# Experts' first layer: two blocks' 64-channel parts side by side in the array's row halves, bias moved into the gelu

## The reference, cut to what matters

```python
xn2 = _layernorm(x, norm2_w, norm2_b).reshape(-1, C)      # 1152 x 192
logits = xn2 @ w_gate
top_vals, top_idx = jax.lax.top_k(logits, 2)
gates = softmax(top_vals)
def body(acc, p):                                          # for each of 8 experts
    w1, bb1, w2, bb2, g = p                                # w1 192 x 768, w2 768 x 192
    h = jax.nn.gelu(xn2 @ w1 + bb1, approximate=False)
    return (acc + g[:, None] * (h @ w2 + bb2), None)
```

## Time and profile before

| what | value |
|---|---|
| median of 3 runs (lowest, highest) | 395.0 us (394.66, 396.63) |
| the profiled execution: its time, its span | 395.83 us, 393.9 us |
| PE, weight loads (PEld), DVE, ACT, POOL busy | 321.1, 284.4, 226.4, 170.8, 82.3 us |
| mean granted clock of TensorE | 0.888 of full |
| chain that ended last, by engine | PE 63%, DVE 17%, DMA 7%, ACT 5% |
| experts' loop, from the first L1424 to the end of the span | 292.08 to 393.9 us |

### The profile page before, as it was taken

How to read it: one execution, slowest core, us unless ns; L and a number is a source line. 1 busy time by engine, 2 the same in 40 slices (tenths; PEclk the granted TensorE clock), 3 DMA queues, 4 the chain that set the end, 5 groups by cost and what they waited for, 6 DMA issues and landing times.

```text
span 393.9 us, 6349 instructions
## 1 busy us (share of the span) xinstructions
PE 321.1 (81%) x2177; PEld 284.4 (72%) x2177; DVE 226.4 (57%) x543; ACT 170.8 (43%) x408; POOL 82.3 (21%) x79
## 2 busy tenths in 40 slices
PE   8869506680979899999998896649599999999990
PEld 6849404460768797887986674639499999999980
DVE  1718998999989746553473875568422332322230
ACT  0154402404624277798847964116233333333320
POOL 9310002010000101010010000000405555554631
PEclk9989956796698999999999997557689999999996
DMA  8950000000000003443039588000222222222322
GB/s 279 360 146 0 1 0 0 0 2 0 1 2 1 0 2 95 122 135 84 24 80 262 165 206 237 17 22 1 55 86 42 42 41 43 42 40 42 51 23 22
DMA packets 20555, 27.27 MB, mean 69 GB/s; under 512 B 3458, under 2 KB 15570, under 8 KB 20522
## 3 DMA queue, kind: packets, MB, share of 16 engines
q1 hardware_dynamic: 16634, 22.80, 20.4%
q0 software_dynamic: 3888, 4.03, 7.0%
HBM read 22.05 MB, written 4.77 MB: 68 GB/s over the span
## 4 chain that ended last, share of the span: by engine, by line
PE 63%; DVE 17%; DMA 7%; ACT 5%; issue 4%; POOL 1%; SPq 1%; DVEq 0%; ACTq 0%; POOLq 0%
PE banks L1424 9%; PE banks L1214 9%; PE banks L1215 9%; PE banks L1411 7%; PE banks L1413 7%; PE banks L1284 6%; DMA vs<-v_scratch 4%; PE banks L1237 3%; ACT patch L757 2%; PE banks L1247 2%; DVE arena L979 1%; PE banks L1385 1%; PE banks L1335 1%; PE banks L1308 1%; PE banks L1208 1%
## 5 line engine op out<-in xcount | busy, mean ns | idle before, releaser
L579 POOL TENSOR_TENSOR rs<-va,consts 96x6 f32<-96x6 f32 (+1 forms) x16 | 17.8, 1114 | 222.8 <-DVE va L890 129.0
L833 ACT ACTIVATE ffn<-banks 128x384 f32<-128x384 f32 x40 | 19.6, 491 | 61.3 <-PE banks L1413 60.5
L600 POOL DMA_INDIRECT out<-s,ffn x20 | 32.4, 1620 | 49.5 <-DVE s L1175 41.3
L1424 PE MATMUL banks<-arena,ffn 128*128 x240 | 42.1, 326 | 0.0
L1175 DVE TENSOR_SCALAR s<-banks,ffn 128x192 f32<-128x192 f32 x20 | 8.3, 417 | 57.4 <-PE banks L1424 47.9
L1424 PEld LDWEIGHTS banks<-arena,ffn 128*128 128x128 f32 x240 | 38.5, 190 | 0.0
L1214 PE MATMUL banks<-ht,kvrw 128*128 128x288 f32 x40 | 17.9, 538 | 19.9 <-DVE h L876 14.7
L1247 PE MATMUL banks<-consts,xh 96*128 96x96 f32 (+1 forms) x96 | 12.9, 280 | 19.1 <-DVEq L914 17.8
L590 POOL DMA_INDIRECT vs<-xh_scratch,ffn x21 | 21.2, 1008 | 32.4 <-DVE ffn L1154 26.3
L1284 PE MATMUL banks<-rvw,ffn 128*96 128x192 f32 x144 | 26.4, 335 | 1.0 <-ACT ffn L729 1.0
L1214 PEld LDWEIGHTS banks<-ht,kvrw 128*128 128x128 f32 x40 | 9.5, 252 | 23.4 <-issue 17.8
(11 more groups left out here) (215 smaller groups left out, 756.2 us busy)
## 6 DMA issues: line engine op xcount, KB each, us to landing
arena<-in_w SPq DMA_DIRECT2D x8, 576.0 KB, 8.1
patch<-in_xp SPq DMA_DIRECT2D x12, 288.0 KB, 5.9
arena<-in_w1a SPq DMA_DIRECT2D x8, 384.0 KB, 6.3
vs<-v_scratch SPq DMA_DIRECT2D x24, 114.8 KB
arena<-in_w1b SPq DMA_DIRECT2D x8, 195.0 KB
v_scratch<-vt SPq DMA_DIRECT2D x4, 229.5 KB, 3.0
xh_scratch<-xh SPq DMA_DIRECT2D x4, 216.0 KB, 2.4
out<-h SPq DMA_DIRECT2D x1, 864.0 KB, 4.9
```

The costliest lines, as they stand in the source:

```text
L600: pool.indirect_dma_start(out[:, :], bass.IndirectOffsetOnAxis(ap=IS[:, j:j + 1], axis=0), YG[j % 2], None, compute_op=ALU.add).then_inc(s ...
L833: freed(A(HST[j % 2][:, 384 * i:384 * (i + 1)], ps[:, 0:384], ACT.Gelu), job)
L1424: ins = mm(ps[:, 0:C], HST[j % 2][:, 128 * k:128 * (k + 1)], W2[:, bass.ds(e, 1), C * k:C * (k + 1)], start=(k == 0), stop=(k == HB - 1))
```

## The change

The 64-channel parts of two hidden blocks (m and m + 3) lie in partitions 0 to 63 and 64 to 127 of W1B, and so do two copies of the tokens' last 64 channels in XT. `up` first makes all six 128-channel matmuls (now L1427), then three pairs of 64-channel matmuls (now L1432), one of each pair in rows 0 to 63 of the array and the other in rows 64 to 127, into the two banks. For the second copy the scratch rows are 256 channels wide (a second store per group), and the gathered rows too. The bias is loaded as 48 rows, transposed once by PE (job `b1`), copied with the weights (6 columns, behind the old tile's gelu), and added by six ACTIVATEs of 128 columns (now L841) in place of two of 384. The job `b1` moves all later jobs by one bank.

```diff
-                    load("w1b", W1B[0:C1 + 1, e, :], w1b[:, e, :])
+                    for r in range(2):
+                        load("w1b", W1B[C1 * r:C1 * (r + 1), e, :], w1b[0:C1, e, HID // 2 * r:HID // 2 * (r + 1)])
...
+                if n_experts < E and upto == E:
+                    load("b1", B1ROWS, w1b[C1, :, :].rearrange("e (m p) -> (e m) p", p=128))
...
-                    sp.dma_start(xh_dram[GT * g:GT * (g + 1), :].rearrange("(t p) c -> p t c", p=T),
-                                 XH[:, GTILES * (g % 2):GTILES * (g % 2 + 1), :]).then_inc(xh_stored[g], 16)
+                    sp.dma_start(rows[:, :, 0:C], xh).then_inc(xh_stored[g], 16)
+                    sp.dma_start(rows[:, :, C:256], xh[:, :, 128:C]).then_inc(xh_stored[g], 16)
...
-                freed(A(XT[j % 2][0:C1, 1, :], ps[0:C1, 128:256], ACT.Identity, bias=chan_("n2_b", 1), scale=chan_("n2_w", 1)), job)
+                freed(A(XT[j % 2][:, 1, :], ps[:, 128:256], ACT.Identity, bias=chan_("n2_b", 1, 0, 128), scale=chan_("n2_w", 1, 0, 128)), job)
...
-                    freed(A(HST[j % 2][:, 384 * i:384 * (i + 1)], ps[:, 0:384], ACT.Gelu), job)
+                    for m in range(3 * i, 3 * i + 3):
+                        ins = A(HST[j % 2][:, 128 * m:128 * (m + 1)], ps[:, 128 * (m % 3):128 * (m % 3 + 1)], ACT.Gelu,
+                                bias=WE[j % 2][:, HID + HID // 2 + m:HID + HID // 2 + m + 1])
+                    freed(ins, job)
...
-                ch.then(CP(we[:, 0:1, :], W1A[:, bass.ds(e, 1), :]))
-                ch.step(CP(we[0:C1 + 1, 1:2, :], W1B[0:C1 + 1, bass.ds(e, 1), :]))
+                ch.then(CP(we[:, 0:HID].unsqueeze(1), W1A[:, bass.ds(e, 1), :]))
+                ch.then(CP(we[:, HID:h1].unsqueeze(1), W1B[:, bass.ds(e, 1), :]))
+                if j >= 2:
+                    taken(dve, ("h", j - 2, 1))
+                ch.step(CP(we[:, h1:h1 + HB].unsqueeze(1), B1[:, bass.ds(e, 1), :]))
...
+            ps = full(dve, ("b1",))
+            freed(CP(B1.rearrange("p e m -> p (e m)"), ps[:, 0:E * HB]), ("b1",))
+            taken(dve, ("b1",))
...
+            pe.wait_ge(loaded["b1"], 16)
+            ps = begin(("b1",))
+            end(pe.transpose(ps[:, 0:E * HB], B1ROWS, ident[0:E * HB, 0:E * HB]), ("b1",))
...
-                for i in range(2):
-                    ps = begin(("h", j, i))
-                    for k in range(3):
-                        at_ = 384 * i + 128 * k
-                        h = ps[:, 128 * k:128 * (k + 1)]
-                        mm(h, WE[j % 2][:, 0, at_:at_ + 128], XT[j % 2][:, 0, :], start=True, stop=False)
-
-                        ins = mm(h, WE[j % 2][0:C1 + 1, 1, at_:at_ + 128], XT[j % 2][0:C1 + 1, 1, :], start=False, stop=True)
-                    end(ins, ("h", j, i))
+                we, xt = WE[j % 2], XT[j % 2]
+                ps = [begin(("h", j, i)) for i in range(2)]
+                for m in range(HB):
+                    mm(ps[m // 3][:, 128 * (m % 3):128 * (m % 3 + 1)], we[:, 128 * m:128 * (m + 1)], xt[:, 0, :], start=(m % 3 == 0), stop=False)
+
+                for k in range(3):
+                    for i in range(2):
+                        r = slice(C1 * i, C1 * (i + 1))
+                        ins = mm(ps[i][:, 128 * k:128 * (k + 1)], we[r, HID + 128 * k:HID + 128 * (k + 1)], xt[r, 1, :], start=False, stop=(k == 2))
+                        if k == 2:
+                            end(ins, ("h", j, i))
```

More of the change, by code:

```diff
@@ L158, in moe_jobs @@
 def moe_jobs():
-    out = [("rank",), ("gturn",)] + [("b2", t) for t in range(0, TILES, 2)] + [("list",)]
+    out = [("rank",), ("gturn",)] + [("b2", t) for t in range(0, TILES, 2)] + [("b1",), ("list",)]
     out += [("xt", 0), ("xt", 1), ("h", 0, 0), ("h", 0, 1)]
@@ L208, in build @@
         W1A = arena[:, 0:E * HID].rearrange("p (e n) -> p e n", e=E)
-        W1B = arena[:, E * HID:2 * E * HID].rearrange("p (e n) -> p e n", e=E)
+        W1B = arena[:, E * HID:E * HID + E * HID // 2].rearrange("p (e n) -> p e n", e=E)
+        B1ROWS = arena[0:E * HB, E * HID + E * HID // 2:E * HID + E * HID // 2 + 128]
+        B1 = arena[:, 2 * E * HID - E * HB:2 * E * HID].rearrange("p (e m) -> p e m", e=E)
         W2 = arena[:, 2 * E * HID:ARENA].rearrange("p (e n) -> p e n", e=E)
@@ L264, in build @@
         names = ["chan", "const", "tokw", "tokb", "kvrw", "wow", "kfw", "rfw", "vfw", "qkvw", "projw",
-                 "gatew", "b2", "w1a", "w1b", "w2"]
+                 "gatew", "b2", "w1a", "w1b", "b1", "w2"]
         loaded = {n: sem("loaded_" + n) for n in names}
@@ L356, in xh_free @@
                 if kk == "g":
-                    eng.wait_ge(xh_stored[gg], 16)
+                    eng.wait_ge(xh_stored[gg], 32)
         class Chain:
@@ L440, in fcarve @@
             return ffn[:, fat[0] - n:fat[0]]
-        XG = [vs_[:, C * i:C * (i + 1)] for i in range(3)]
+        XG = [vs_[:, 256 * i:256 * (i + 1)] for i in range(3)]
         YG = [S[:, i, 0:C] for i in range(2)]
@@ L449, in build @@
         HST = [fcarve(HID) for _ in range(2)]
-        WE = [x.rearrange("p (b n) -> p b n", b=2) for x in (rvw[:, :], fcarve(2 * HID))]
+        WE = [rvw[:, 0:HID + HID // 2 + HB], fcarve(HID + HID // 2 + HB)]
         v_dram = nc.dram_tensor("v_scratch", [TOK, NH * HW], F32).ap()
-        xh_dram = nc.dram_tensor("xh_scratch", [TOK, C], F32).ap()
+        xh_dram = nc.dram_tensor("xh_scratch", [TOK, 256], F32).ap()
         block = ctx.enter_context(nc.Block())
@@ L509, in _ @@
                     normalised(sp, step[1:])
-                    sp.dma_start(xh_dram[GT * g:GT * (g + 1), :].rearrange("(t p) c -> p t c", p=T),
-                                 XH[:, GTILES * (g % 2):GTILES * (g % 2 + 1), :]).then_inc(xh_stored[g], 16)
+                    rows = xh_dram[GT * g:GT * (g + 1), :].rearrange("(t p) c -> p t c", p=T)
+                    xh = XH[:, GTILES * (g % 2):GTILES * (g % 2 + 1), :]
+                    sp.dma_start(rows[:, :, 0:C], xh).then_inc(xh_stored[g], 16)
+                    sp.dma_start(rows[:, :, C:256], xh[:, :, 128:C]).then_inc(xh_stored[g], 16)
                 if kind == "vt":
@@ L584, in _ @@
             for g in range(G):
-                pool.wait_ge(xh_stored[g], 16)
+                pool.wait_ge(xh_stored[g], 32)
             def gather(j):
@@ L1134, in _ @@
             ch.then(dve.memset(O[:, 0, :], 0.0))
-            for j in range(2):
-                ch.then(dve.memset(XT[j][C1:C1 + 1, 1, :], 1.0))
             def weights(j):
@@ L1142, in weights @@
                 we = WE[j % 2]
-                ch.then(CP(we[:, 0:1, :], W1A[:, bass.ds(e, 1), :]))
-                ch.step(CP(we[0:C1 + 1, 1:2, :], W1B[0:C1 + 1, bass.ds(e, 1), :]))
+                h1 = HID + HID // 2
+                ch.then(CP(we[:, 0:HID].unsqueeze(1), W1A[:, bass.ds(e, 1), :]))
[3 more added lines that the diff above has]
+                ch.step(CP(we[:, h1:h1 + HB].unsqueeze(1), B1[:, bass.ds(e, 1), :]))
                 dve.sem_inc(we_ready, 1)
@@ L1149, in _ @@
             dve.wait_ge(loaded["w1a"], 16 * E)
-            dve.wait_ge(loaded["w1b"], 16 * E)
+            dve.wait_ge(loaded["w1b"], 32 * E)
+            ps = full(dve, ("b1",))
+            freed(CP(B1.rearrange("p e m -> p (e m)"), ps[:, 0:E * HB]), ("b1",))
+            taken(dve, ("b1",))
             weights(0)
@@ L1386, in _ @@
             end(ins, ("list",))
-            for n in ("w1a", "w1b", "w2"):
-                pe.wait_ge(loaded[n], 16 * E)
+            for n, k in (("w1a", 1), ("w1b", 2), ("w2", 1)):
+                pe.wait_ge(loaded[n], 16 * k * E)
             def tile_expert(j):
@@ L1398, in turn_tokens @@
                 pe.transpose(ps[:, 0:128], XG[j % 3][:, 0:128], ident)
-                end(pe.transpose(ps[0:C1, 128:256], XG[j % 3][:, 128:C], ident), ("xt", j))
+                end(pe.transpose(ps[:, 128:256], XG[j % 3][:, 128:256], ident), ("xt", j))
             def up(j):
```

## The result

**397.0 us** (median of 20 executions, 394.5 to 400.9) against 394.3 for the kernel before (20 executions): a ratio of 1.017, 95% interval 1.012 to 1.022. Slower. Ratios and intervals here leave out executions more than 1.5% above the fastest of their kernel, which leaves 5 of the 20 before and 19 of the 20 after, so 1.017 stands too high: the medians of all 20 and 20 give 1.007. The same kernel gave 1.0111 (1.0047 to 1.0176) when it ran again among the experiments, and with one buffer more, which does not touch its loop, 1.0078 (1.0037 to 1.0120). Over the three the loss is 2.7 to 3.6 us between medians, so 0.7 to 0.9%. The forecast was 394.7 and "the same".

The account below looks back on a forecast made before the run. TensorE bounds the kernel at 4.85 us a tile; after the change a loop through ScalarE would, at 4.86. Start -0.25, 17 x 0.01, end -0.27 sum to -0.35 us: 394.7 us (the same), range 390.5 to 400.0.

Parts of the forecast that it names:

- the ring: Steady loop, end of one `up` to the next through ScalarE's gelus and norm copies: 4.86 us, setting the period.
- TensorE's own period, 4.58: TensorE's work per tile: 4.85 us, less 0.67 for overlapping pairs, plus 0.40 for switching between whole array and halves.
- Six gelus, 1.51: ScalarE after `up`: six 128-column gelus with pointer bias, 0.25 us from start to start, 1.51 us in all.
- the second rival: Gelus follow each other at 0.292 us, lengthening the loop through ScalarE to 5.11 us: 398.9 us, slower; chance 0.15.
- 0.03 to the first gelu: Steady loop: the first gelu starts 0.03 us after the end of `up`.
- 0.45 for the second [norm copy]: ScalarE, behind the six gelus: the second norm copy takes 0.45 us.
- To TensorE, start and `up`, 2.52: After the second norm copy: 0.04 us to TensorE, 0.27 to start it again, 2.21 for `up` itself.
- At the end ... -0.27: End of the loop: `up(19)`, a transpose and `down(18)` run at TensorE's 4.58 us, saving 0.27 us.
- The start, -0.25: Start of the loop: `up(2)` starts 0.25 us earlier than before, with the additions ahead of it counted in.
- Rival 1: Switching costs little with row halves: `up` 2.01 to 2.1 us, 390.9 us, faster; chance 0.27 including milder forms.
- Rival 3: Row halves don't overlap: `up` 2.88 us, loop through ScalarE 5.53, about 408 us; chance 0.08.
- Rival 4: Lower clock while TensorE waits, or later `v` transfer moving others: 2 to 5 us lost, about 398; chance 0.08.

Follow-up runs that it names:

- pairs first: Changed kernel with the three pairs of 64-channel matmuls ahead of the six whole ones in `up`: 391.17 us, 0.9891 of the kernel before; repeated, 390.62 us, 0.9936.
- norm copies first and four buffers: Changed kernel with next tile's norm copies ahead of the gelus, transposes ahead of `up`, fourth gather buffer, gathers a tile earlier: 391.53 us, 0.9938 of the kernel before.
- loads and rows: Kernel before with w1b in two transfers per expert, second `xh` store and 1024-byte gathered rows: 1.0027 and 0.9993; loads alone 1.0033, rows alone 0.9896.
- the first repair: Changed kernel with next tile's norm copies ahead of the gelus and transposes ahead of `up`, three gather buffers: 403.5 us, 1.0240 of the kernel before.

## Why the prediction was wrong

The range (390.5 to 400.0) held the time; the forecast of "the same" did not. The mechanism was named: the ring through ScalarE would replace TensorE as the bound. It failed in the size of the ring's terms, on which everything hung, because the forecast was a ring of 4.86 within 0.01 us of the old period.

- *TensorE's own period, 4.58.* Nearly right: in the change's own order it is 4.53 (two gelus, or six without a pointer), so the two switches cost 4.53 - 4.85 + 0.67 = 0.35 us, where 0.40 was read from column halves in the earlier trace rows. With pairs first, or with norm copies first and four buffers, it is 4.57, so 0.39. The pairs' 0.67 holds for row halves.
- *Six gelus, 1.51.* Right: 1.52. The fit of PSUM rows was the right row: 128 columns with a pointer from PSUM start 0.25 us apart, and the second rival, at 0.292, falls. The estimate of 0.294 us from the figures of the Trainium skill (ScalarE: Activation LUTs, "What ACT_TABLE_LOAD costs") does not agree with this row.
- *"0.03 to the first gelu".* Wrong: in the timeline `up`'s last pass ends at 335.09 (334.15 + 0.94) and the gelu starts at 335.18, so 0.09. It is not the pointer: in the kernel before with six gelus, which have one too, three of them start 0.03 us behind the end of `up`. The chain shows an extra step of 0.02 at the semaphore and 0.05 of issue. Two waits stand ahead of the first gelu of a tile, one ahead of the gelu that the earlier trace rows show; whether the extra wait takes the 0.06 was not tried.
- *"0.45 for the second [norm copy]".* Wrong: 0.50. The copy is now 128 partitions high instead of 64, but that is not the reason. With norm copies first and four buffers the same 128x128 copy does not stand behind the gelus, and takes 0.45 us:

```profile
301.82 0.45 ACT L835 ACTIVATE ffn<-banks,chans 128x128 f32<-128x128 f32 x1
```

Behind two gelus of 384 columns it takes 0.465 us, behind six of 128 0.50, with a pointer or without. So the length of this copy goes by what stands ahead of it; why was not tried.
- *To TensorE, start and `up`, 2.52.* Right: 337.54 to 340.06 is 2.52.
- So the ring is 4.86 + 0.06 + 0.05 = 4.97. Over the tiles from the first `down` to the 19th this is 89.49 - 87.30 = **+2.19 us**, where the sum had 17 x 0.01 - 0.27 = -0.10.
- *"At the end ... -0.27".* Wrong in kind: `up(19)` waits in the ring like the others, and the last two `down`s of the row lie 4.97 apart, 0.12 more than before instead of 0.27 less.
- *The start, -0.25.* The sign is right: from the first gather to the first `down` 12.52 us against 13.04, so -0.5. The working is not: "2.50" for the ring without `up` should be 4.86 - 2.21 = 2.65 by the prediction's own terms. What lies ahead of the first gather is not in the -0.5.
- *Rival 1 (the switch is cheap)*: false, the switches cost 0.35. *Rival 3 (no overlap)*: false. *Rival 4*: the clock in the loop stayed at 1.00.

By the trace the loss is thus +2.2 - 0.5 + 0.2 (the end behind the last `down`) = 1.9 us. The medians say 2.7 to 3.6. The loads and rows do not supply the rest. Whether it is the bias's load and transpose, DVE's changed order, or chance (single executions of the kernel before lie between 387.6 and 397.9) **stays open**. The traces do not settle it: the first gather starts at 274.2 to 278.9 us in the six with the loop of before (mean 277.0) and at 276.2 to 280.8 in the eleven with the change (mean 277.7), and a difference of 1 us cannot be read through that.

The prediction also said that POOL would be late "if the period fell below about 4 us". That limit was too low: a late scatter starts 0.79 us after the one before has landed, and some transfers take 4 to 5 us, so tiles were late already at 4.57. And it didn't look at the gather behind the scatter, which the first repair ran into.

## What to carry to other kernels

When a matmul is made shorter by making the operations behind it smaller and more, add up the whole loop through both engines, term by term and in the new shapes, and ask when each PSUM bank closes. Here the same matmuls in another order (the split ones first) turned about 1% slower into about 1% faster, because half of ScalarE's work could then start during `up`. When two kernels share a period that should differ, look whether they share a bound: a chain that names one engine can hide a wait of another. Before moving a consumer earlier, look at what stands ahead of its producer in the queue; one buffer more may be the other half of the edit. And a forecast that balances two limits within 0.01 us is a coin toss: price both sides to 0.05 or say so.

## What the runs showed of the hardware

- A pointer bias costs ScalarE 0.081 us on a 128x128 gelu from PSUM (375 against 294 ns), while the columns cost little: 384 of them without a pointer start 0.39 us apart.
- fp32 passes in different row halves run side by side, 0.11 us per pair, and the second half's passes start while three of the first half's are still to come, even if the program has them one after the other. Going from the whole array to halves and back costs 0.35 us per tile where the transposes follow the halves, 0.39 where the halves stand in front or `down` follows them at once.
- The same 128x128 copy from PSUM took 0.45 us behind another copy alone, 0.465 behind two gelus of 384 columns and 0.50 behind six of 128.
- A transfer that adds rows into memory took about 3.5 us in most cases (3.41 and 3.53 above) but 4 to 5 in others in the same loop (4.62 and 5.05 above). What stretches it was not tried.
